# First feed-forward of a two-layer transformer step as one unrolled stream over the batches, its latents taken from the transposed normalised input

## The chip, the cores and the metric

The kernel runs on one core of a Trainium2 chip. The metric is device time in microseconds (us) of one launch. The times shown are the median of three runs and one profiled execution, from which every duration below is read.

## The reference, cut to what matters

The input x is 8 batches of 512 tokens of width 256. The layer adds to x an attention branch and a feed-forward branch, both fed by the layer norm of x. The attention branch norms its input a second time, scales and shifts it and projects it to two latents of width 128. A second layer (linear attention and routed experts) follows and isn't touched.

```
xn = _layernorm(x, axis=-1)
# attention branch, start (its input here is xn)
h = (x - mu) * jax.lax.rsqrt(var + LN_EPS) * ln_scale + ln_bias
c_q = h @ w_down_q.T
c_kv = h @ w_down_kv.T
# feed-forward branch
bw1 = _binarize(w1)          # mean |w| of each row times sign(w)
h = jnp.einsum('bsd,hd->bsh', x, bw1) + b1
h = jax.nn.gelu(h, approximate=False)
bw2 = _binarize(w2)
out = jnp.einsum('bsh,dh->bsd', h, bw2) + b2
```

## The kernel before

The program is a row of stages. Stage f (`stage_f`) comes first: for each batch b it computes `part` = x + xn + the feed-forward of xn, and the two latents, and writes both to HBM; stage a (`stage_a`, the attention) reads them. A barrier over all engines stands between the stages, so stage a starts its own loads only when stage f has ended.

The engines are TensorE (PE in the profile), VectorE (DVE), ScalarE (ACT), GpSimd (POOL) and SyncE (SP, which issues the loads and stores). Each runs its own instruction list in order and waits on semaphores. fp32 values that TensorE multiplies are split in a high part, rounded by ScalarE, and a low part, the rest, made by VectorE or GpSimd (`xT_hi`, `xT_lo`, `g_hi`, `g_lo`, `hT_hi`, `hT_lo`, `wd_hi`, `wd_lo`).

One batch, in `one(more)` of each engine, is:

- TensorE transposes h, the twice normed input, in 8 pieces into the banks `pX`; then 8 column blocks m of the up product, 4 matmuls each, into a ring of three banks `pU`; then the latents, 12 matmuls (`product`, lines 101 to 103), into `pX`; then the down product over 4 token tiles t, 64 matmuls of 256 columns (line 432) into two banks `pY`. At t = 2 it transposes the next batch's xn, for which it waits on the norm of that batch.
- ScalarE applies Gelu twice to each `pU` bank (into `g` and `g_hi`), rounds the latents, takes two square roots for the next batch's two norms (line 293), each behind the norm that feeds it, and rounds `xT_hi`. Square root and Gelu need different tables, each with a load.
- VectorE makes `hT` from the transposed h, the 8 `g_lo`, the latents' low parts, then the two norms of the next batch (`layer_norm`, lines 114 to 127), `xT_lo`, and, once the down product is there, `y` = `pY` times `alpha2` and `out` = `y` + `base`.
- GpSimd makes `base` = x + xn + b2 and splits hT.

There is one copy of each buffer. A batch ends in a meeting: each engine adds one to `arrived` and waits for `go` (`meet`); SP, which has issued the store of `part`, waits for all four and for the latents' store, clears 20-odd semaphores one by one and lets all go (`lead`, lines 90 to 97). The batches are a loop of seven turns and one copy behind it. Ahead of the loop all weights are loaded on one semaphore (`loaded`, 112), and signs and means are taken when the last has come. Behind it `part` of batch 7 is stored, and then a spare copy of latents 0 is made.

## Time and profile before

| | |
|---|---|
| median of 3 runs | 2234.28 us (2234.1 to 2235.52) |
| profiled execution | 2242.25 us, its span 2240.6 us |
| TensorE busy | 1922.1 us, 86% |
| VectorE busy | 1301.0 us, 58% |
| ScalarE busy | 895.0 us, 40% |
| GpSimd busy | 1328.1 us, 59% |
| mean granted TensorE clock | 0.94 of full |
| stage f | 0 to 277.31 us (the first load of stage a is issued then) |

Busy shares are means over stages with different limits; stage f takes an eighth of the span and is read by itself in the rows below. A row of the time line gives the start, the length, the engine, the line, the operation, what it writes and reads, and in brackets how long the engine had been idle and who released it. Matmuls overlap, so their pace is the distance of their starts, not their length. The granted clock is 1.00 at 2.4 GHz and 0.5 at 1.2 GHz.

### The profile page before, as it was taken

Reading aid. Unit: us, or ns where it says so; the run is one execution under the profiler, and the core shown is the slowest. Engines: PE = TensorE matmul, PEld = TensorE weight load, DVE = VectorE, ACT = ScalarE, POOL = GpSimd, SP = SyncE. Lnnn points to the kernel's source line nnn. Section 1 sums busy time; section 2 is a strip of 40 time slices with the busy share of each in tenths; the row PEclk is TensorE's granted clock in tenths of the full one; section 3 lists DMA queues with packets and bytes.
Section 4 is the critical chain, followed back from the end, with each engine's and each line's share of the span. In section 5 each row is a group of like instructions: output and inputs, shape, how many; then the busy total and the mean of one; then the engine's idle time right before and its main releaser. Section 6 shows DMA issues by size and latency. Waiting matters only on the chain. (4 is left out here: it accounts for less than half of the span.)

```text
span 2240.6 us, 35323 instructions
## 1 busy us (share of the span) xinstructions
PE 1922.1 (86%) x12804; PEld 1333.1 (59%) x12804; DVE 1301.0 (58%) x1857; ACT 895.0 (40%) x1536; POOL 1328.1 (59%) x860
## 2 busy tenths in 40 slices
PE   5777649999999999999999964888885699998798
PEld 4666524454454545454454533666764699998798
DVE  6666436666656565666656523676663466565343
ACT  4554324433434343433434212333321355554454
POOL 2333228886868687887878632544544566666533
PEclk9888869999999999999999977999997899999899
DMA  3212231323222231323232213122213433323122
GB/s 102 75 56 75 86 106 40 76 48 95 57 67 69 50 93 34 95 48 95 57 85 58 57 29 126 32 70 77 61 57 105 133 81 81 77 51 107 29 45 42
DMA packets 81606, 158.63 MB, mean 71 GB/s; under 512 B 14496, under 2 KB 63520, under 8 KB 75552
## 3 DMA queue, kind: packets, MB, share of 16 engines
q1 hardware_dynamic: 66464, 133.40, 21.2%
q0 software_dynamic: 14592, 18.40, 5.0%
q10 hardware_dynamic: 432, 5.24, 0.6%
q8 instruction: 76, 1.25, 0.2%
q14 instruction: 42, 0.34, 0.1%
HBM read 80.84 MB, written 44.17 MB: 56 GB/s over the span
## 5 line engine op out<-in xcount | busy, mean ns | idle before, releaser
L916 ACT ACTIVATE a_pr<-a_pT 128x1024 f32<-128x1024 f32 x256 | 262.1, 1024 | 432.4 <-PE a_pT L739 432.4
L949 POOL TENSOR_TENSOR a_total<-a_total,a_pr 128x1024 f32<-128x1024 f32 x128 | 321.0, 2507 | 149.9 <-ACT a_pr L916 149.5
L821 DVE TENSOR_REDUCE a_row_max<-a_pG 128x2 f32<-128x1024 f32 x256 | 309.2, 1220 | 148.7 <-PE a_pG L713 148.6
L1832 DVE TENSOR_TENSOR c_h_lo<-c_h,c_h_hi 128x256 fp32r<-128x256 f32 x288 | 213.0, 757 | 195.0 <-ACT c_h_hi L1811 176.9
L752 PE MATMUL a_pA<-a_pr,a_v 128*64 128x512 f32 x1024 | 277.0, 619 | 0.1
L1811 ACT ACTIVATE c_h<-c_pU,c_b_c 128x256 f32<-128x256 f32 x288 | 138.8, 482 | 235.1 <-PE c_pU L103 234.5
L949 POOL TENSOR_TENSOR a_total<-a_pr 128x1024 f32<-128x1024 f32 x64 | 151.7, 2370 | 59.7 <-ACT a_pr L916 59.5
L930 POOL TENSOR_TENSOR a_by_cos<-a_by_cos,a_swapped 128x1024 f32<-128x1024 f32 x64 | 155.1, 2424 | 46.3 <-DMA a_swapped<-a_by_sin 46.2
L815 DVE TENSOR_TENSOR a_by_sin<-a_pG,a_sin 128x1024 f32<-128x1024 f32 x64 | 78.4, 1225 | 141.9 <-PE a_pG L103 136.9
L937 POOL TENSOR_TENSOR a_qk_lo<-a_by_cos,a_qk_hi 128x1024 fp32r<-128x1024 f32 x64 | 158.9, 2483 | 2.3 <-ACT a_qk_hi L886 2.3
L1868 POOL DMA_INDIRECT out_x<-c_y,c_ids x72 | 114.7, 1593 | 41.4 <-DVE c_y L1840 22.7
L1811 ACT ACTIVATE c_h_hi<-c_pU,c_b_c 128x256 fp32r<-128x256 f32 x288 | 138.0, 479 | 0.0
L713 PEld LDWEIGHTS a_pG<-a_qk_hi 64*128 64x128 f32 x512 | 46.1, 187 | 150.4 <-issue 89.6
L770 PE MATMUL a_pG<-a_wo,a_att 128*128 128x256 f32 x512 | 119.9, 389 | 15.0 <-DVE a_att L842 15.0
L713 PE MATMUL a_pG<-a_qk_hi 64*128 64x512 f32 x512 | 121.3, 491 | 10.9 <-ACTq L897 6.4
L101 PE MATMUL c_pY<-d_w_hi,c_h_lo 128*128 128x256 f32 x368 | 107.0, 291 | 19.5 <-DVE c_h_lo L1832 18.8
L101 PE MATMUL c_pU<-c_xT_hi,d_w_lo 128*128 128x256 f32 x368 | 109.4, 297 | 12.2 <-remote 11.0
L886 ACT CAST a_qk_hi<-a_by_cos 128x1024 fp32r<-128x1024 f32 x64 | 67.1, 1048 | 126.7 <-POOL a_by_cos L930 126.7
L770 PEld LDWEIGHTS a_pG<-a_wo,a_att 128*128 128x128 f32 x512 | 96.1, 192 | 34.9 <-issue 19.3
L734 PE MATMUL a_pT<-a_qk_hi,a_qk_lo 64*128 64x512 f32 x512 | 113.1, 436 | 1.3 <-ACT a_pr L916 1.0
L273 POOL TENSOR_TENSOR f_base<-f_x_t,f_xn 128x1024 f32<-128x1024 f32 x8 | 18.9, 2363 | 151.2 <-SPq L96 151.2
L739 PE MATMUL a_pT<-a_neg_max,a_ones 64*128 64x512 f32 x512 | 108.3, 417 | 0.0
(248 smaller groups left out, 5072.7 us busy)
## 6 DMA issues: line engine op xcount, KB each, us to landing
a_swapped<-a_by_sin SPq DMA_DIRECT2D x256, 128.0 KB, 2.3
a_inv_by_head<-mid_inverses SPq DMA_DIRECT2D x32, 512.0 KB, 6.0
c_x_t<-mid_rows SPq DMA_DIRECT2D x37, 272.0 KB, 2.8
mid_latents<-f_c_parts SPq DMA_DIRECT2D x8, 1024.0 KB, 3.9
a_latent_parts<-mid_latents SPq DMA_DIRECT2D x8, 1024.0 KB, 7.2
d_raw<-in_weights SPq DMA_DIRECT2D x3, 2048.0 KB, 8.4
c_raw<-in_weights SPq DMA_DIRECT2D x3, 2048.0 KB, 8.1
f_x_t<-in_x SPq DMA_DIRECT2D x8, 512.0 KB, 3.9
```

Source lines behind the costliest of these rows:

```text
L101: nc.tensor.matmul(out, l_lo, r_hi, start=start, stop=False, **kw)
L713: last = nc.tensor.matmul(pair[:, h, :], qk_hi[rows, u % RQ, 0, t * P:(t + 1) * P], qk_hi[rows, u % RQ, 1, :], start=True, stop=True)
L752: last = nc.tensor.matmul(pA[64 * h:64 * h + 64, :], v[:, t, p, h, :], pr[:, n % RP, h, :], start=(t == 0), stop=(t == NT - 1))
L770: last = nc.tensor.matmul(pair[:, 0, 0:D], att[:, (NP * b + p) % RA, ts], wo[:, p * D:(p + 1) * D], start=(p == 0), stop=(p == NP - 1))
L821: nc.vector.reduce_max(row_max[:, u % 2, :, t], pair[:], AX.X).then_inc(read, 1)
L916: nc.scalar.activation(pr[:, n % RP, :, :], pT[:], ACT.Exp, scale=SCALE).then_inc(exp_done, 1)
L930: nc.gpsimd.tensor_tensor(by_cos[:, u % 2, :, :], by_cos[:, u % 2, :, :], swapped[:], ALU.add).then_inc(rope_done, 1)
L937: nc.gpsimd.tensor_tensor(qk_lo[:, u % RQ, :, :], by_cos[:, u % 2, :, :], qk_hi[:, u % RQ, :, :], ALU.subtract).then_inc(qk_lo_done, 1)
L949: nc.gpsimd.tensor_tensor(total[:, u % 2, :, :], before, pr[:, n % RP, :, :], ALU.add).then_inc(summed, 1)
L1811: nc.scalar.activation(dst[:, m % RH, :], pU[m % RH][:], ACT.Relu, bias=b1_c[:, e, m:m + 1]).then_inc(relu_done[m % RH], 1)
L1832: nc.vector.tensor_tensor(h_lo[:, m % RH, :], h[:, m % RH, :], h_hi[:, m % RH, :], ALU.subtract).then_inc(h_lo_done[m % RH], 1)
L1868: pool.indirect_dma_start(out=out, out_offset=bass.IndirectOffsetOnAxis(ap=ids[:, t:t + 1], axis=0), in_=y[:, t, :], in_offset=None, compu ...
```

## The change

Stage f is written out over the 8 batches with no loop and no meeting. Its semaphores are never cleared while it runs, but count up; VectorE clears all 50 of them at the start of stage a. Inputs, xn, the transposed halves, `g_lo`, `g_hi` and the latents have two buffers, `base` three, `out` four half batches; `g` becomes a ring of three blocks. TensorE alternates: after the up block m of batch b comes a half token tile of the down product of batch b - 1 (`down(b - 1, m)`, 8 matmuls).

The second norm is no longer computed over data. The mean of xn is zero and its variance is var/(var+eps), so h = xn times a number per token. Hence the latents are `wd` (multiplied by ln_scale, `wd_s`) times the xT halves that exist already, then multiplied by that number. The number must be laid along columns: GpSimd makes `diag` (identity times `rstd2[:, 1]`), TensorE multiplies a matrix of ones by it (`spread`, 4 fp32 matmuls), ScalarE copies the result (`cols`), VectorE multiplies (`scale`), and ScalarE and VectorE split the sum with the bias `c_bias`. Both square roots are one instruction (`roots`). What goes is the transposes of h, `hT` and its split. GpSimd takes over the addition that makes `out` (`result`). The loads of the weights are cut in halves with a semaphore each. The spare copy is made after batch 2.

```diff
-                        if t == 2 and more:
-                            pe.wait_ge(c_lo_done, 2)
-                            pe.wait_ge(ln_step, LN_ALL)
-                            transposes(xn, xT_done)
...
+            spent.append(st.lasting(name))
+            return spent[-1]
...
+        x_t = [sb(f"x_t{i}", [P, NT, D]) for i in range(2)]
+        xn = [sb(f"xn{i}", [P, NT, D]) for i in range(2)]
+        RB = 3
+        base = [sb(f"base{i}", [P, NT, D]) for i in range(RB)]
+        y = [sb(f"y{i}", [P, 2, D]) for i in range(2)]
+        RO = 4
+        out = [sb(f"out{i}", [P, 2, D]) for i in range(RO)]
...
+        RG = 3
+        g = sb("g", [P, RG, S])
...
+        pT = [bank(f"pT{c}") for c in range(KC)]
         pU = [bank(f"pU{i}") for i in range(3)]
         pY = [bank(f"pY{i}", (P, 2, D)) for i in range(2)]
+        pC = bank("pC")
...
+                sp.dma_start(x_t[0][:], tokens(x, 0)).then_inc(x_in[0], 16)
                 sp.dma_start(ident[:], ident_d).then_inc(ident_in, 16)
+                sp.dma_start(w1s[:, :, 0:half], turned[:, :, 0:half]).then_inc(w1s_in[0], 16)
+                sp.dma_start(w1r[:, 0:MC // 2, :], rows[:, 0:MC // 2, :]).then_inc(w1r_in[0], 16)
+                sp.dma_start(b1_c[:], b1).then_inc(b1_in, 16)
+                sp.dma_start(ln[:], ln_sb).then_inc(ln_in, 16)
+                sp.dma_start(wd[:], wd_t).then_inc(wd_in, 16)
+                sp.dma_start(w1s[:, :, half:], turned[:, :, half:]).then_inc(w1s_in[1], 16)
+                sp.dma_start(w1r[:, MC // 2:, :], rows[:, MC // 2:, :]).then_inc(w1r_in[1], 16)
+                sp.dma_start(x_t[1][:], tokens(x, 1)).then_inc(x_in[1], 16)
...
+                def spread_base(b):
+
+                    pool.wait_ge(norm, normed(b, ROOTS))
+                    if b:
+                        pool.wait_ge(spread_done, b)
+                    else:
+                        pool.wait_ge(ident_in, 16)
+                    for t in range(NT):
+                        nc.gpsimd.tensor_scalar(diag[:, t, :], ident[:], rstd2[:, 1, t:t + 1], None,
+                                                ALU.mult).then_inc(diag_done, 1)
+                    pool.wait_ge(norm, normed(b, XN))
+                    if b >= RB:
+                        pool.wait_ge(out_done, 2 * (b - RB) + 2)
+                    nc.gpsimd.tensor_tensor(base[b % RB][:], x_t[b % 2][:], xn[b % 2][:],
+                                            ALU.add).then_inc(sum_done, 1)
+                    if not b:
+                        pool.wait_ge(b2_in, 16 * NT)
+                    pool.wait_ge(sum_done, b + 1)
+                    nc.gpsimd.tensor_tensor(base[b % RB][:], base[b % RB][:], b2_rows[:],
+                                            ALU.add).then_inc(base_done, 1)
+
+                def result(q):
+                    b, i = q // 2, q % 2
+                    pool.wait_ge(y_done, q + 1)
+                    pool.wait_ge(base_done, b + 1)
+                    if q >= RO:
+                        pool.wait_ge(stored[q % RO], 16 * (q // RO))
+                    nc.gpsimd.tensor_tensor(out[q % RO][:], y[q % 2][:], base[b % RB][:, 2 * i:2 * i + 2, :],
+                                            ALU.add).then_inc(out_done, 1)
...
+                spread_base(0)
+                for b in range(B + 2):
+                    if b >= 2:
+                        result(2 * (b - 2) + 1)
+                    if b + 1 < B:
+                        spread_base(b + 1)
+                    if 1 <= b <= B:
+                        result(2 * (b - 1))
+                pool.wait_ge(out_done, 2 * B)
...
+                def roots(b):
+                    act.wait_ge(norm, normed(b, VAR2))
+                    nc.scalar.activation(std2[:], var2[:], ACT.Sqrt).then_inc(root, 1)
...
+                roots(0)
+                signs(0)
+                x_high(0)
+                act.wait_ge(b1_in, 16)
+                for b in range(B):
                     for m in range(MC):
+                        k = MC * b + m
...
+                        if k >= RG:
+                            act.wait_ge(g_lo_done, k + 1 - RG)
...
+                        if not b:
+                            if m == 0:
+                                signs(1)
+                            if m == 2:
+                                columns(0)
+                            if m == 4:
+                                act.wait_ge(w2s_in, 16)
+                                nc.scalar.activation(w2abs[:], w2s[:], ACT.Abs).then_inc(w2abs_done, 1)
+                            if m == 6:
+                                nc.scalar.activation(sign2[:], w2s[:], ACT.Sign).then_inc(sign2_done, 1)
+                        if b + 1 < B:
+                            if m == 0:
+                                roots(b + 1)
+                            if m == 4:
+                                x_high(b + 1)
+                            if m == 7:
+                                columns(b + 1)
+                        if m == 5:
+                            latent_high(b, 0)
+                        if m == 7:
+                            latent_high(b, 1)
...
+                def scale(b, i):
+                    dve.wait_ge(c_done, 2 * b + i + 1)
+                    dve.wait_ge(cols_done, b + 1)
+                    if b:
+                        dve.wait_ge(c_lo_done, 2 * b + i - 1)
+                    nc.vector.tensor_tensor(scaled[i][:], pC[:], cols[b % 2][:], ALU.mult).then_inc(scaled_done, 1)
+
+                def latent_low(b, i):
+                    dve.wait_ge(c_hi_done, 2 * b + i + 1)
+                    nc.vector.scalar_tensor_tensor(out=c_parts[b % 2][:, 2 + i, :], in0=scaled[i][:],
+                                                   scalar=c_bias[:, i:i + 1], in1=c_parts[b % 2][:, i, :],
+                                                   op0=ALU.add, op1=ALU.subtract).then_inc(c_lo_done, 1)
+
+                def weigh(q):
+                    dve.wait_ge(down_done, q + 1)
+                    if q >= 2:
+                        dve.wait_ge(out_done, q - 1)
+                    nc.vector.tensor_tensor(y[q % 2][:], pY[q % 2][:], alpha2[:], ALU.mult).then_inc(y_done, 1)
...
+                moments(0)
+                normalise(0)
+                means(0)
+                x_low(0)
+                moments(1)
+                means(1)
...
+                        if b >= 2 and m == 0:
+                            weigh(2 * (b - 2) + 1)
+                        if b + 1 < B and m == 1:
+                            normalise(b + 1)
+                        if m == 3:
+                            scale(b, 0)
+                        if b and m == 4:
+                            weigh(2 * (b - 1))
+                        if m == 5:
+                            if b + 1 < B:
+                                x_low(b + 1)
+                            latent_low(b, 0)
+                        if m == 6:
+                            scale(b, 1)
+                        if m == 7:
+                            latent_low(b, 1)
+                            if b + 2 < B:
+                                moments(b + 2)
...
+                def transposes(b):
+                    pe.wait_ge(norm, normed(b, XN))
+                    if b:
+                        pe.wait_ge(cols_done, b)
...
+                def spread(b):
+
+                    pe.wait_ge(diag_done, NT * (b + 1))
+                    pe.wait_ge(xT_lo_done, KC * b + 1)
+                    for t in range(NT):
+                        last = nc.tensor.matmul(pT[0][:, t * P:(t + 1) * P], ones[:], diag[:, t, :],
+                                                start=True, stop=True)
+                    last.then_inc(spread_done, 1)
...
+                        up(b, m)
+                        if b:
+                            down(b - 1, m)
+                        if not b and m == 0:
+                            pe.wait_ge(ln_in, 16)
+                            pe.wait_ge(wd_in, 16)
+                            for i in range(2):
+                                for c in range(KC):
+                                    last = nc.tensor.matmul(pC[:, i:i + 1], wd[:, (2 * c + i) * P:(2 * c + i + 1) * P],
+                                                            ln[:, 1, c:c + 1], start=(c == 0), stop=(c == KC - 1))
+                            last.then_inc(c_bias_made, 1)
+                            pe.wait_ge(ones_set, 1)
+                            spread(0)
+                        if m == 2:
+                            latents_of(b, 0)
+                        if b + 1 < B and m == 3:
+                            transposes(b + 1)
+                        if m == 5:
+                            latents_of(b, 1)
+                        if b + 1 < B and m == 6:
+                            spread(b + 1)
...
+                    for s in spent:
+                        dve.sem_clear(s)
```

The instructions as they now stand, at three places. VectorE before, the end of one batch and the start of the next (L367 makes `y`, L373 `out`, L87 is the meeting):

```order
L344 TENSOR_TENSOR f_xT_lo<-f_pX,f_xT_hi 128x512 [waits f_xT_hi_done] x2
L367 TENSOR_TENSOR f_y<-f_pY,f_alpha 128x512 [waits f_down_done,f_ln_step,f_xT_lo_done]
L367 TENSOR_TENSOR f_y<-f_pY,f_alpha 128x512 [waits f_down_done]
L373 TENSOR_TENSOR f_out<-f_y,f_base 128x512 [waits f_y_done,f_out_free,f_base_done]
L373 TENSOR_TENSOR f_out<-f_y,f_base 128x512 [waits f_y_done]
L87 ISA [waits f_out_done,f_c_lo_done,f_go1]
L392 REGISTER_ALU
L392 COMPARE_AND_BRANCH
L352 TENSOR_SCALAR f_hT<-f_pX,f_ln 128x512 [waits f_h_done] x2
L356 TENSOR_TENSOR f_g_lo<-f_g,f_g_hi 128x512 [waits f_gelu_done] x8
```

VectorE now, the first blocks of batch 3 (`f_g_lo1` is its low half, `f_y1` belongs to batch 1, `f_xn0` to batch 4):

```order
L526 TENSOR_TENSOR f_g_lo1<-f_g,f_g_hi1 128x512 [waits f_gelu_done]
L512 TENSOR_TENSOR f_y1<-f_pY1,f_alpha2 128x512 [waits f_out_done,f_down_done]
L526 TENSOR_TENSOR f_g_lo1<-f_g,f_g_hi1 128x512 [waits f_gelu_done]
L469 RECIPROCAL f_rstd2<-f_std2 128x8 [waits f_diag_done,f_root]
L471 SCALAR_TENSOR_TENSOR f_shift<-f_mean_var,f_rstd2 128x4 [waits f_norm]
L477 TENSOR_SCALAR f_xn0<-f_x_t0,f_rstd2,f_shift 128x256 [waits f_sum_done,f_norm]
L477 TENSOR_SCALAR f_xn0<-f_x_t0,f_rstd2,f_shift 128x256 x3
L526 TENSOR_TENSOR f_g_lo1<-f_g,f_g_hi1 128x512 [waits f_gelu_done] x2
L500 TENSOR_TENSOR f_scaled0<-f_pC,f_cols1 128x512 [waits f_c_lo_done,f_cols_done,f_c_done]
L526 TENSOR_TENSOR f_g_lo1<-f_g,f_g_hi1 128x512 [waits f_gelu_done]
```

The norm of the next batch stands between the second and third `g_lo`, no longer ahead of a meeting, and the out addition is gone from this engine.

TensorE before, from the end of the down product over the meeting to the next batch:

```order
L432 MATMUL f_pY<-f_sign,f_g_lo 128x256
L432 MATMUL f_pY<-f_sign,f_g_hi 128x256
L87 ISA [waits f_down_done,f_go0]
L453 REGISTER_ALU
L453 COMPARE_AND_BRANCH
L401 MATMUL f_pX<-f_ident,f_h 128x128 x8
L412 MATMUL f_pU<-f_xT_lo,f_sign 128x512
L413 MATMUL f_pU<-f_xT_hi,f_sign 128x512
L412 MATMUL f_pU<-f_xT_lo,f_sign 128x512
```

TensorE now, at the end of slot m = 3 of a batch:

```order
L272 MATMUL f_pY<-f_sign,f_g_lo 128x256
L272 MATMUL f_pY<-f_sign,f_g_hi 128x256
L569 MATMUL f_pT<-f_ident,f_xn 128x128 [waits f_cols_done,f_norm]
L569 MATMUL f_pT<-f_ident,f_xn 128x128 x7
L600 MATMUL f_pU<-f_xT_lo,f_sign 128x512 [waits f_gelu_done]
L601 MATMUL f_pU<-f_xT_hi,f_sign 128x512
L600 MATMUL f_pU<-f_xT_lo,f_sign 128x512
L601 MATMUL f_pU<-f_xT_hi,f_sign 128x512
L272 MATMUL f_pY<-f_sign,f_g_lo 128x256 [waits f_y_done]
```

The transposes of the next batch now stand between two up blocks, and wait for `norm` (xn ready).

ScalarE now, from the end of one batch (`cols` and the latents' second high part) over the start of the next:

```order
L392 COPY f_cols<-f_pT 128x512 [waits f_spread_done]
L398 ACTIVATE f_c_parts<-f_scaled,f_c_bias 128x512 [waits f_scaled_done]
L422 ACTIVATE f_g<-f_pU,f_b_c,f_alpha 128x512 [waits f_g_lo_done,f_up_done]
L422 ACTIVATE f_g_hi<-f_pU,f_b_c,f_alpha 128x512
L383 ACT_TABLE_LOAD
L383 ACTIVATE f_std<-f_var 128x8 [waits f_norm]
L422 ACT_TABLE_LOAD [waits f_g_lo_done]
L422 ACTIVATE f_g<-f_pU,f_b_c,f_alpha 128x512 [waits f_up_done]
L422 ACTIVATE f_g_hi<-f_pU,f_b_c,f_alpha 128x512
L422 ACTIVATE f_g<-f_pU,f_b_c,f_alpha 128x512 [waits f_g_lo_done,f_up_done]
```

The square root with its two table loads has moved from the end of the batch to between the first and the second Gelu pair.

## Rows read from the trace of the kernel before

**Rows 1.** Page, part 5: GpSimd's first instruction of each batch.

```profile
L273 POOL TENSOR_TENSOR f_base<-f_x_t,f_xn 128x1024 f32<-128x1024 f32 x8 | 18.9, 2363 | 151.2 <-SPq L96 151.2
```

**Rows 2.** Time line of PE, 88 to 125 us, one turn of the loop.

```profile
100.96 0.40 PE L101 MATMUL f_pX<-f_hT_hi,f_wd_lo 128*128 128x512 f32 x1
...
103.73 0.28 PE L432 MATMUL f_pY<-f_sign,f_g_lo 128*128 128x256 f32 x1
...
107.25 0.28 PE L432 MATMUL f_pY<-f_sign,f_g_hi 128*128 128x256 f32 x1
109.95 1.94 PE L401 MATMUL f_pX<-f_ident,f_xn 128*128 128x128 f32 x8 [2.43 <-DVE f_xn L127]
...
111.91 0.42 PE L432 MATMUL f_pY<-f_sign,f_g_hi 128*128 128x256 f32 x1
112.12 0.41 PE L432 MATMUL f_pY<-f_sign,f_g_lo 128*128 128x256 f32 x1
...
120.65 1.97 PE L401 MATMUL f_pX<-f_ident,f_h 128*128 128x128 f32 x8 [4.34 <-SPq L94]
```

**Rows 3.** Stage table: one turn; busy us, granted clock (PEclk).

```profile
120.60:151.60 31.00, 23.63 (x125) 19.82 (x126) 20.40 (x48) 15.98 (x25) 10.68 (x10) 0.89 0.19 70
```

**Rows 4.** Time line of PE, 20 to 32 us, ahead of batch 0.

```profile
20.68 5.56 PE L447 MATMUL f_pY<-f_w2abs,f_ones 128*128 128x256 f32 x16 [9.62 <-ACT f_w2abs L323]
28.65 1.07 PE L401 MATMUL f_pX<-f_ident,f_h 128*128 128x128 f32 x8 [2.42 <-SPq L94]
```

**Rows 5.** Time line of DVE, 90 to 126 us, same turn.

```profile
104.53 1.28 DVE L360 TENSOR_TENSOR f_c_parts<-f_pX,f_c_parts 128x512 fp32r<-128x512 f32 x2
105.73 1.40 DVE L114 BATCH_NORM_STATS2 f_stats<-f_x_t 128x6 f32<-128x256 f32 x4
...
108.43 1.38 DVE L127 TENSOR_SCALAR f_xn<-f_x_t,f_small 128x256 f32<-128x256 f32 x4
```

**Rows 6.** Time line of ACT, 90 to 126 us, same turn.

```profile
102.36 0.86 ACT L304 ACTIVATE f_g<-f_pU,f_b_c,f_alpha 128x512 f32<-128x512 f32 x1
103.03 0.86 ACT L304 ACTIVATE f_g_hi<-f_pU,f_b_c,f_alpha 128x512 fp32r<-128x512 f32 x1
...
104.87 1.28 ACT L293 ACT_TABLE_LOAD   x1
...
112.01 1.06 ACT L298 CAST f_xT_hi<-f_pX 128x512 fp32r<-128x512 f32 x2
```

**Rows 7.** f_g_lo by tile: count, then min/median/max ns.

```profile
L356 DVE TENSOR_TENSOR f_g_lo<-f_g,f_g_hi x64: 691/718/1840, 32.2 to 259.2; 128x512 fp32r<-128x512 f32 x64
```

**Rows 8.** Time line of DVE, 150 to 165 us.

```profile
157.60 1.04 DVE L356 TENSOR_TENSOR f_g_lo<-f_g,f_g_hi 128x512 fp32r<-128x512 f32 x1 [0.65 <-ACT f_g_hi L304]
```

**Rows 9.** Time line of POOL, 150 to 165 us.

```profile
154.49 1.29 POOL L278 TENSOR_TENSOR f_hT_lo<-f_hT,f_hT_hi 128x512 fp32r<-128x512 f32 x1
...
156.42 1.68 POOL L278 TENSOR_TENSOR f_hT_lo<-f_hT,f_hT_hi 128x512 fp32r<-128x512 f32 x1
```

**Rows 10.** Groups of POOL's instructions over the whole span.

```profile
L1590 POOL TENSOR_SCALAR d_own<-b_qT,b_own 128x512 f32<-128x512 f32 x32 | 50.4, 1587 | 16.0 <-DVE b_qT L1357 15.6
```

**Rows 11.** Time line of all engines, 0 to 29 us, start-up.

```profile
4.89 1.41 DVE L114 BATCH_NORM_STATS2 f_stats<-f_x_t 128x6 f32<-128x256 f32 x4 [4.89 <-DMA f_x_t<-in_x]
...
15.02 1.91 ACT L321 ACTIVATE f_sign<-f_w1s 128x2048 fp32r<-128x2048 f32 x1 [2.79 <-DMA f_ln<-in_ln_sb]
```

**Rows 12.** Time line of PE, 264 to 280 us.

```profile
266.17 0.28 PE L432 MATMUL f_pY<-f_sign,f_g_hi 128*128 128x256 f32 x1
```

**Rows 13.** Time line of SP, 264 to 280 us, the stage's end.

```profile
268.40 0.38 SPq L241 DMA_DIRECT2D mid_part<-f_out  x1
271.37 0.69 SPq L261 DMA_DIRECT2D mid_latents<-mid_latents  x1
277.31 0.37 SPq L520 DMA_DIRECT2D a_raw_q<-in_wq_t  x1
```

**Rows 14.** Time line of DVE, 276 to 300 us, its first work in stage a.

```profile
289.98 1.23 DVE L534 TENSOR_TENSOR a_wq_lo<-a_raw_q,a_wq_hi 128x1024 fp32r<-128x1024 f32 x1 [21.61 <-ACT a_wq_hi L528]
```

More of the change, by code:

```diff
@@ L184, in stage_f @@
[L184 to L189 removed]
+        inv_var = sb("inv_var", [P, NT])
+        share = sb("share", [P, NT])
+        var2 = sb("var2", [P, 2, NT])
+        std2 = sb("std2", [P, 2, NT])
+        rstd2 = sb("rstd2", [P, 2, NT])
+        shift = sb("shift", [P, NT])
+        xT_hi = [sb(f"xT_hi{i}", [P, KC, S], F32R) for i in range(2)]
@@ L251, in _ @@
[L251 to L261 removed]
+                half = FF // 2
@@ new lines, in up @@
+                def up(b, m):
+                    k = MC * b + m
+                    if k >= 3:
+                        pe.wait_ge(gelu_done, 2 * (k - 2))
+                    for c in range(KC):
+                        w = sign1[:, c, m * P:(m + 1) * P]
+                        nc.tensor.matmul(pU[k % 3][:], w, xT_lo[b % 2][:, c, :], start=(c == 0), stop=False)
+                        last = nc.tensor.matmul(pU[k % 3][:], w, xT_hi[b % 2][:, c, :], start=False,
+                                                stop=(c == KC - 1))
+                    last.then_inc(up_done, 1)
```

460 lines of the change are left out of this document (231 added, 229 removed).

## The prediction

> **What bounds the kernel now.** I read the page first. Its costliest groups are of later stages, but one row of stage f stands out: the first instruction of GpSimd in each batch had an idle time of 151.2 us before it in 8 times, and SyncE's line 96, the `go` of the meeting, ended it [rows 1]. So the stage is paced by its meetings, not by an engine. The stage table of one turn says the same: of 31.0 us TensorE is busy 23.6, VectorE 20.4, ScalarE 16.0, GpSimd 10.7, and TensorE's granted clock is 0.89 [rows 3]. Then the time line of TensorE over one turn. Two holes stand in it: 2.43 us for the norm of the next batch in the middle of the down product, and 4.34 us for the meeting [rows 2]. Behind the first hole the matmuls of 256 columns start 0.21 us apart (111.91 and 112.12), against 0.1135 before it (31 steps from 103.73 to 107.25): the lower of the two clock levels, 1.2 GHz.
>
> **The change, first a batch in the steady state.** What TensorE must do, at full clock. The 12 latent matmuls of 512 columns run from 100.96 to 103.73, 0.231 us each [rows 2]. The 32 up matmuls have that shape: 7.4 us. Down: 64 by 0.1135, 7.3 us. Latents: 2.8 us, as before. Transposes of xn: 8 took 1.07 us with their tail [rows 4], 0.85 net. Those of h (0.85) go. New is `spread`, 4 fp32 matmuls of 128 columns. Before has fp32 matmuls of 256 columns, 8 instructions (16 records) in 5.56 us [rows 4], 0.70 us each; half as many columns give 0.35 each, 1.4 us; at the best clock perhaps half. I take 0.9. Sum 19.3 us, with no hole in it. That is the floor of a batch.
>
> ScalarE: a Gelu is 0.67 us from start to start, 16 make 10.7; two table loads 1.28 each, 2.6; `xT_hi` 1.06 [rows 6]; three more passes of 512 columns at about 0.58, 1.7; the root 0.2. Sum 16.3.
>
> VectorE: 8 `g_lo` at 0.69 [rows 7] make 5.5; eight passes of the same size (`xT_lo`, `scale`, the latents' low part, `weigh`, two each), at 0.64 apart [rows 5], 5.1; statistics from 105.73 to the root, with two more tiny steps, 2.5; reciprocal, shift and xn 1.8 (1.38 of it xn [rows 5]). Sum 14.9. GpSimd: two additions of 1024 columns at 2.36 [rows 1], two of 512 at 1.29 [rows 9], and 4 `diag`; a tensor_scalar of 512 columns takes 1.59 [rows 10], so 128 columns about 0.45 and four 1.8. Sum 9.1. So TensorE is the engine with the most to do.
>
> But VectorE and GpSimd get in each other's way. A `g_lo` takes 0.69 us at best and up to 1.84 [rows 7]; the one at 157.60 took 1.04 and ended only 0.5 us after GpSimd's instruction of 156.42, which itself took 1.68 where its like at 154.49 took 1.29 [rows 8, 9]. I read: one waits for the whole instruction of the other. The Trainium skill says this outright (SBUF — State Buffer, section "SBUF: two separate sides"): the pair of ports that both share is an exclusive lock, and the one that comes second is blocked for a full instruction. By that rule the batch is the walk below, without it the floor of 19.3; the trace bears the lock out.
>
> Now walk one batch, time 0 at TensorE's first up block. A slot (up block, then half a down tile) is 0.93 + 0.91 = 1.84 us; latents (1.4) follow in slots 2 and 5, transposes in slot 3, `spread` in slot 6. ScalarE ends the previous batch at 1.6 (last Gelu pair 0.5, `cols`, latents). Then Gelu pair 0 to 2.9, load and root to 4.4, load to 5.7, pair 1 to 7.1. VectorE has finished the statistics of the batch after next meanwhile; `g_lo` 1 to 7.8, or 8.2 if the `out` addition (GpSimd, 6.3 to 7.6) holds it; then reciprocal, shift and xn to 10.2. TensorE wants to transpose at 3.68 + 1.84 + 1.4 + 1.84 = 8.8. **First stall: 1.4 us.** Behind xn come GpSimd's two additions of 2.36, with `g_lo` 2 and 3 squeezed in: `g_lo` 2 to 10.8, GpSimd to 13.2, `g_lo` 3 to 13.9, GpSimd to 16.2 (`scale` reads PSUM and goes through), `g_lo` 4 to 16.9, `weigh` to 17.5, `g_lo` 5 to 18.2, the first `xT_lo` to 18.9. TensorE wants `spread`, which overwrites the bank `xT_lo` reads, at 18.0. **Second stall: 0.9 us.** The rest fits: VectorE ends its last `g_lo` about 1.1 us into the next batch, as assumed. A batch is 19.3 + 1.4 + 0.9 = 21.6, with semaphore hops 21.8 us, against 31.0 now.
>
> The ring `g` of three blocks lets ScalarE be at most three ahead of VectorE; in the walk `g_lo` 3 is done at 13.9 and Gelu 6 comes at 17.1, so it isn't reached. Loads, stores and latents are issued on SP long before they are used.
>
> **The start.** x 0 has landed at 4.89, all the 4 MB of loads at 15.0 [rows 11]. The norm now takes the shorter way (one set of statistics): xn at 9.5, transposes to 11.2, `xT_hi` and `xT_lo` to 12.4 with half the signs in between. First up block 12.4 to 14.1 at the low clock, first Gelu 14.2. ScalarE then has the longest list: 8 Gelu pairs 10.7, signs and absolute values 1.91 each for a full matrix [rows 11], so half of sign1, `w2abs` and sign2 make 4.8, loads and root 2.8, `xT_hi`, `cols`, latents 2.8: 21 us, to 35. VectorE adds a latents part, statistics of batch 2 and `alpha2` behind it: 39.2. TensorE waits for `alpha2` there and starts batch 1's slots. x 1 is the ninth load (some 3.3 of 4 MB), so `g_lo` 0 starts only near 17.4; the ring of three covers it, barely. Before, batch 0 started at 28.65 [rows 4] and took a turn: 59.7.
>
> **The end.** Batches 1 to 6 are whole slots: 6 by 21.8 = 130.8, to 170.0. Batch 7 has no transposes, `spread` or norm: 18.5, to 188.5. Its down product stands alone, 7.3, after a wait of 1.3 for the last `g_lo`: 197.1. Then `weigh` 0.7, the addition on GpSimd 1.3, the store (268.40 to 271.37, 3.0 [rows 13]), 0.5 of hops and barrier: 202.6. Before, from TensorE's last matmul at 266.17 [rows 12] to stage a's first load at 277.31 [rows 13] it was 11.1, since the spare copy came behind the store (271.37 to 277.31, 5.9). The 50 semaphores that VectorE clears in stage a: a whole meeting with 23 clears kept TensorE idle 4.34 [rows 2], so 50 cost 9.4 at most; VectorE has nothing to do there from 277.31 to 289.98 [rows 13, 14], 12.7 us. Without that cover they would cost up to 9.4.
>
> **Sum.** 277.3 - 202.6 = 74.7 us off the profiled span of 2240.6: 2165.9, profiled time 2167.6. The profiled execution (2242.25) stood 8 us above the median of 2234.28, so I predict 2234.3 - 74.7 = 2159.6, 2160 us. Stage a begins behind a barrier, so nothing later changes, and nothing there gives it back.
>
> **The rivals.**
>
> *Floor* (0.27). The stalls are covered: the table loads fall in holes, or GpSimd's additions come late enough. Then a batch is 19.3 to 20.3, 6 of them 9 to 15 less: 2145 to 2151. For it: each stall is about 1 us in a walk of 20 steps. Against: the root, two loads and xn are one chain of over 6 us.
>
> *Clock* (0.19). TensorE falls to 1.2 GHz behind stalls. The evidence is split: a hole of 2.42 us at 28.65 left the 8 transposes at 1.07 us (full clock), one of 2.43 at 109.95 made them 1.94 and slowed what followed [rows 2, 4]. One fall costs 0.9 there and 7 matmuls by 0.1, about 1.6 us; one or two in each batch give 23.4 to 25, 6.5 batches by 1.6 to 3.2: 2170 to 2181. The Trainium skill (TensorE: Matmul & The Clock Gate, section "What's actually happening") says that the throttled state is the default and activity releases it, which speaks for a denser stream as good for the clock.
>
> *Slower* (0.03). The clock stays at 1.2 GHz through the stage, as alternating short groups with waits might do: 44 matmuls of 512 columns at twice 0.231, 64 at 0.213, transposes 1.9, `spread` 1.8: 37.6 us. Seven batches are 263; with 39.2 ahead, and 1.3, 14.0 and 5.5 behind, the stage ends at 323, 46 us later: 2280. It decides where 7 batches exceed 277.3 - 39.2 - 1.3 - 14.0 - 5.5 = 217, 31.0 us each.
>
> *No gain* (0.01). The stage is held by something unseen (a full ring, fetching a straight program): 31 us a batch. The waits named in the trace are all meeting and norm, which go.
>
> The rest (0.50) is my forecast, 21 to 23 us a batch, 2154 to 2168 alone. The start may be 5 us off either way, as all but its durations is reckoned. The range takes in floor and clock: 2141 to 2182. Within 0.2% (4.5 us) nothing could be told from no change; that and slower hold 0.04 together, faster 0.96.
>
> **What would show it.** Stage a's first load near 203 instead of 277; no idle time that SP ended in stage f; up blocks of one column block about 21.8 us apart; before the `f_xn` transposes an idle of 1 to 1.5 us ended by VectorE, before the `f_diag` matmuls about 1 us ended by `xT_lo`; `g_lo` longer on average than 0.93 us where it meets GpSimd; TensorE's clock 0.97 or more from 45 us on. I would be wrong if ScalarE's Gelu shows as what TensorE waits for, or if TensorE starts batch 1 much later than 39.

## The result, and the profile after

The changed kernel took 2168.36 us (median of four runs, 2162.8 to 2169.34), the kernel before 2234.19 beside it: a ratio of 0.970, 95% interval 0.9683 to 0.9717, so it is faster. 2160 was predicted, with 2141 to 2182 as the range. Of the 74.3 us forecast from the median, 65.8 came. The profiled execution took 2169.34 (span 2167.7), and its stage f ends, by stage a's first load, at 210.51 us instead of 277.31 [rows 13]: 66.8 us earlier, where 74.7 was predicted.

The stage table. Each row is a stretch: busy time and instructions of TensorE, its weight load, VectorE, ScalarE and GpSimd, then granted clock, DMA share and GB/s. The first two are the start, the third is batch 1, the fourth is one of the five batches behind it, which differ by less than 0.1 us, then batch 7 and the down product alone:

```profile
0.00:13.00 13.00, 1.94 (x8) 1.57 (x8) 6.90 (x22) 3.62 (x5) 4.10 (x9) 1.00 0.87 291
13.00:49.30 36.30, 24.60 (x92) 19.74 (x93) 20.94 (x49) 23.01 (x29) 15.04 (x13) 0.86 0.28 93
49.30:71.00 21.70, 21.54 (x125) 19.22 (x126) 13.46 (x19) 15.17 (x22) 9.91 (x7) 0.92 0.12 37
...
114.40:136.10 21.70, 19.96 (x125) 17.63 (x125) 15.67 (x34) 16.56 (x25) 11.44 (x8) 1.00 0.27 98
...
180.00:198.00 18.00, 18.00 (x114) 16.10 (x113) 10.01 (x14) 13.29 (x21) 3.10 (x2) 1.00 0.22 88
198.00:210.50 12.50, 7.41 (x61) 7.00 (x59) 3.35 (x5) 0.70 (x2) 3.82 (x3) 1.00 0.39 148
```

Against the turn of 31.0 us with clock 0.89 [rows 3], a batch is now 21.7 us with clock 1.00 (batch 1: 0.92), and TensorE is busy 92% of it. The 36.3 us of the second row are what went worse than forecast: TensorE stands idle 11.7 us there, at a clock of 0.86.

The time line of TensorE after, its stops in order: the start, one steady batch, the end. In brackets stand the idle time ahead and who ended it.

```profile
26.49 0.76 PE L101 MATMUL f_pC<-f_xT_hi,f_wd_lo 128*128 128x512 f32 x1 [5.46 <-DVE f_c_bias L530]
...
39.55 1.39 PE L578 MATMUL f_pT<-f_diag,f_ones 128*128 128x128 f32 x8 [3.42 <-DVE f_xT_lo L483]
...
42.44 4.24 PE L648 MATMUL f_pY<-f_w2abs,f_ones 128*128 128x256 f32 x16
49.32 0.47 PE L600 MATMUL f_pU<-f_xT_lo,f_sign 128*128 128x512 f32 x1 [2.64 <-issue]
...
103.32 1.09 PE L569 MATMUL f_pT<-f_ident,f_xn 128*128 128x128 f32 x8 [1.65 <-DVE f_xn L477]
...
111.14 0.28 PE L272 MATMUL f_pY<-f_sign,f_g_hi 128*128 128x256 f32 x1
111.51 1.13 PE L578 MATMUL f_pT<-f_diag,f_ones 128*128 128x128 f32 x8
...
179.61 0.40 PE L600 MATMUL f_pU<-f_xT_lo,f_sign 128*128 128x512 f32 x1
...
197.38 0.28 PE L272 MATMUL f_pY<-f_sign,f_g_lo 128*128 128x256 f32 x1
...
198.87 0.39 PE L272 MATMUL f_pY<-f_sign,f_g_lo 128*128 128x256 f32 x1 [0.37 <-DVE f_g_lo L526]
```

The holes of 2.43 and 4.34 us in each turn [rows 2] are gone, and no idle time on TensorE is ended by SP. Batch 1 begins at 49.32 and batch 7 at 179.61: six batches in 130.3 us, 21.7 each. The transposes after a stop of 1.65 us take 1.09 us, as at full clock [rows 4]. `spread` begins 0.37 us after the start of the last down matmul, some 0.25 more than the usual step of 0.12.

VectorE and GpSimd of the same batch:

```profile
100.78 0.69 DVE L526 TENSOR_TENSOR f_g_lo<-f_g,f_g_hi 128x512 fp32r<-128x512 f32 x1 [1.84 <-ACT f_g_hi L422]
...
101.83 1.44 DVE L477 TENSOR_SCALAR f_xn<-f_x_t,f_rstd,f_shift 128x256 f32<-128x256 f32 x4
...
106.85 1.08 DVE L526 TENSOR_TENSOR f_g_lo<-f_g,f_g_hi 128x512 fp32r<-128x512 f32 x1 [1.70 <-ACT f_g_hi L422]
...
109.17 1.60 DVE L526 TENSOR_TENSOR f_g_lo<-f_g,f_g_hi 128x512 fp32r<-128x512 f32 x1 [0.63 <-ACT f_g_hi L422]
```

```profile
101.69 3.34 POOL L336 TENSOR_SCALAR f_diag<-f_ident,f_rstd 128x128 f32<-128x128 f32 x4 [1.38 <-DVE f_rstd L469]
105.00 2.39 POOL L341 TENSOR_TENSOR f_base<-f_x_t,f_xn 128x1024 f32<-128x1024 f32 x1
107.46 2.75 POOL L346 TENSOR_TENSOR f_base<-f_base,f_b_rows 128x1024 f32<-128x1024 f32 x1
```

xn waits behind `g_lo` 1, which waits for Gelu pair 1: that is the 1.65 us stop. On ScalarE, Gelu pair 1 follows the square root, and the root itself stood 0.73 us for VectorE's statistics, which the walk took to be done by then:

```profile
97.78 0.21 ACT L383 ACTIVATE f_std<-f_var 128x8 f32<-128x8 f32 x1 [0.73 <-DVE f_var L463]
```

 The two longer `g_lo` end 0.5 to 0.6 us after GpSimd's additions (107.39, 110.21), not when their own 0.69 us would be over.

### The profile page after: what moved, and what is told of

Read it like the earlier page. It is cut to its first block and busy times, and to the rows that moved or that the text cites. A ratio compares the mean times of both kernels' runs of the same rounds, so it can differ in the third digit from the quotient of the medians.

```text
span 2167.7 us, 35007 instructions
## 1 busy us (share of the span) xinstructions
PE 1893.2 (87%) x12812; PEld 1316.4 (61%) x12812; DVE 1261.0 (58%) x1748; ACT 900.6 (42%) x1537; POOL 1331.8 (61%) x854
## 5 line engine op out<-in xcount | busy, mean ns | idle before, releaser
L101 PE MATMUL c_pY<-d_w_hi,c_h_lo 128*128 128x256 f32 x368 | 106.4, 289 | 19.3 <-DVE c_h_lo L2036 18.7
L974 PEld LDWEIGHTS a_pG<-a_wo,a_att 128*128 128x128 f32 x512 | 96.0, 192 | 34.9 <-issue 19.3
L102 PE MATMUL c_pU<-c_xT_lo,d_w_hi 128*128 128x256 f32 x368 | 106.4, 289 | 0.0
```

The source lines that it names most:

```text
L101: nc.tensor.matmul(out, l_lo, r_hi, start=start, stop=False, **kw)
L102: nc.tensor.matmul(out, l_hi, r_lo, start=False, stop=False, **kw)
L974: last = nc.tensor.matmul(pair[:, 0, 0:D], att[:, (NP * b + p) % RA, ts], wo[:, p * D:(p + 1) * D], start=(p == 0), stop=(p == NP - 1))
```

## The experiments

In each, the number to compare is stage a's first load, 210.51 us in the changed kernel. The later stages, which no experiment touches, take 1953.0 to 1959.4 us in the profiled executions of the experiments from e1 on (e3 aside), so the whole time says less. The first load is read from one execution of each kernel; TensorE's first transposes, ahead of every edit, begin between 9.56 and 9.76 us in all of them.

### e1: the norm one block earlier

```
-                        if b + 1 < B and m == 1:
+                        if b + 1 < B and m == 0:
                             normalise(b + 1)
```

> One edit to the changed kernel: VectorE's reciprocal, shift and xn of the next batch stand behind the first low half of a batch instead of behind the second, so they no longer wait for the second Gelu pair. Chain theory (TensorE's first stall is xn coming behind root, table load and Gelu pair 1): xn is ready 2 to 2.5 us earlier, the five idle times of 1.65 us before the xn transposes vanish, 8.2 us in all; stage a's first load at 202 to 203 us instead of 210.5, a batch 20.1 instead of 21.8. Rival (VectorE and GpSimd, which block each other, set the batch): xn comes earlier but the idle time moves to the spread matmuls, which wait for the low halves behind GpSimd's additions; a batch stays at 21 or more and stage a starts at 208 or later. Time against before: 0.966 by the first, 0.969 by the second.

Measured: 2160.8 us (five runs), ratio to before 0.9653 (0.9637 to 0.9669). Stage a begins at 206.09, 4.4 us earlier, between the theory and the rival. A batch is 20.8 us (101.41 to 122.18), and the start is 0.9 us longer (the wait for the bias is 6.13 us instead of 5.46). TensorE's stops in a batch:

```profile
101.41 1.09 PE L569 MATMUL f_pT<-f_ident,f_xn 128*128 128x128 f32 x8 [0.23 <-DVE f_xn L477]
110.06 1.13 PE L578 MATMUL f_pT<-f_diag,f_ones 128*128 128x128 f32 x8 [0.53 <-DVE f_xT_lo L483]
```

and why the second one came, on VectorE beside GpSimd:

```profile
98.61 1.26 DVE L471 SCALAR_TENSOR_TENSOR f_shift<-f_mean_var,f_rstd 128x4 f32<-128x4 f32 x1
...
107.27 2.05 DVE L526 TENSOR_TENSOR f_g_lo<-f_g,f_g_hi 128x512 fp32r<-128x512 f32 x1 [0.18 <-ACT f_g_hi L422]
109.24 1.28 DVE L483 TENSOR_TENSOR f_xT_lo<-f_pT,f_xT_hi 128x512 fp32r<-128x512 f32 x2
```

```profile
98.54 1.30 POOL L355 TENSOR_TENSOR f_out<-f_y,f_base 128x512 f32<-128x512 f32 x1 [8.86 <-DVE f_y L512]
...
106.02 2.74 POOL L346 TENSOR_TENSOR f_base<-f_base,f_b_rows 128x1024 f32<-128x1024 f32 x1
108.72 1.72 POOL L355 TENSOR_TENSOR f_out<-f_y,f_base 128x512 f32<-128x512 f32 x1
```

The first stall was the order of VectorE's list: it fell from 1.65 to 0.23 us. Some of it is given back. `f_shift`, 128 by 4 elements and 0.16 us otherwise, took 1.26 and ended with GpSimd's addition; and with everything earlier, `g_lo` 5 and behind it `xT_lo` now come late for `spread`, which is the forecast's second stall.

### e2: the copy of the bias two blocks earlier

```
-                        if not b and m == 2:
+                        if not b and m == 0:
                             dve.wait_ge(c_bias_made, 1)
```

> One edit to the changed kernel: in batch 0 VectorE copies c_bias behind the first low half, not behind the third. Start theory (TensorE's idle of 5.5 us at 21 to 26.5 us is the wait for this copy, since the latents' bank holds the bias until then): latents of batch 0 start near 21.5 instead of 26.5, and as ScalarE sat idle 5.7 us behind it, batch 1 starts 4 to 5 us earlier (44.5 to 45.5 instead of 49.3) and stage a at 205.5 to 206.5. Rival (ScalarE's list of 21 us sets the start): the hole is filled by ScalarE's own work, and less than 2 us comes of it.

Measured: 2159.23 us, one run; stage a at 204.22, 6.3 us earlier, more than either expected. The stop of 5.46 us ahead of the first latents is gone; batch 1 begins at 44.18 instead of 49.32 and meets its xn transposes at 53.67 instead of 59.83. Of these 6.2 us 5.1 come ahead of batch 1 and 1.0 in it, where the clock is now 1.00 and was 0.92. `spread` of batch 1 now waits 3.80 us for `xT_lo`.

### e3 and e3b: the sums of |w2| off the path

`w2abs` goes behind ScalarE's `xT_hi`; the sums go to the other transpose bank, so that batch 1's down product need not wait for them:

```
+                                if not b:
+                                    act.wait_ge(w2s_in, 16)
+                                    nc.scalar.activation(w2abs[:], w2s[:], ACT.Abs).then_inc(w2abs_done, 1)
...
-                            nc.vector.tensor_scalar(alpha2[:, i, :], pY[0][:, 0, :], 1.0 / FF, None,
+                            nc.vector.tensor_scalar(alpha2[:, i, :], pT[1][:, 0:D], 1.0 / FF, None,
...
-                        pe.wait_ge(alpha2_done, 2)
```

> Two edits in batch 0 of the changed kernel: the absolute values of w2 are taken behind the rounding of batch 1's transposed halves instead of ahead, and the 8 matmuls with ones that sum them go to a bank that isn't a down bank, so that TensorE waits for alpha2 only ahead of the next transposes. Start theory: the idle of 3.4 us ahead of spread shrinks by the 1.9 us of the absolute values, and the idle of 2.6 us ahead of batch 1 goes: 4 to 4.5 us, batch 1 at 45, stage a at 206 to 206.5. Rival: TensorE runs into ScalarE's Gelu list instead, and no more than 2 us comes of it.

Measured: 5632.22 us. This says nothing about the edit. The first instructions of TensorE, which are the same in both kernels and lie ahead of anything edited, were already slow; this is the row of e3:

```profile
9.67 3.37 PE L571 MATMUL f_pT<-f_ident,f_xn 128*128 128x128 f32 x8 [9.67 <-DVE f_xn L477]
```

The same eight took 1.94 us when the same kernel was run again:

> The same kernel as in e3_sums_aside, run once more, since there every matmul of the whole program, in stages the edit doesn't touch too, took 1.7 to 3 times as long, from the first transposes on (3.37 us for eight, 1.94 in the unedited kernel, whose instructions up to there are the same). If that belongs to the chip and not to the edit, the time is 2158 to 2168 and the expectations of e3_sums_aside hold: batch 1 at 45 and stage a at 206 to 206.5 (start theory), or less than 2 us gained (rival). If it belongs to the edit, it comes again.

Measured: 2164.16 us; stage a at 208.42, only 2.1 us earlier, as the rival said. The wait for `alpha2` is gone, the one for `xT_lo` is not. On TensorE, ScalarE and VectorE, in this order:

```profile
26.53 0.76 PE L101 MATMUL f_pC<-f_xT_hi,f_wd_lo 128*128 128x512 f32 x1 [4.56 <-DVE f_c_bias L530]
...
40.53 2.05 PE L580 MATMUL f_pT<-f_diag,f_ones 128*128 128x128 f32 x8 [3.80 <-DVE f_xT_lo L483]
```

```profile
34.84 1.07 ACT L388 CAST f_xT_hi<-f_pT 128x512 fp32r<-128x512 f32 x2
35.78 1.94 ACT L438 ACTIVATE f_w2abs<-f_w2s 128x2048 f32<-128x2048 f32 x1
...
38.26 0.80 ACT L422 ACTIVATE f_g_hi<-f_pU,f_b_c,f_alpha 128x512 fp32r<-128x512 f32 x1
```

```profile
39.09 0.69 DVE L526 TENSOR_TENSOR f_g_lo<-f_g,f_g_hi 128x512 fp32r<-128x512 f32 x1 [3.42 <-ACT f_g_hi L422]
39.70 1.28 DVE L483 TENSOR_TENSOR f_xT_lo<-f_pT,f_xT_hi 128x512 fp32r<-128x512 f32 x2
```

`xT_hi` is ready at 35.9, but on VectorE `xT_lo` stands behind `g_lo` 5, and that waits for Gelu pair 5. `w2abs` still stands ahead of that pair, so the edit moved it past `xT_hi` and left it in the way of `xT_lo`. Gelu pairs 3 and 4 ahead of it are late from the bias wait, which this edit leaves. e9 bears this out: it differs from e5 only in that `xT_lo` stands ahead of `g_lo` 5, and its `spread` of batch 1 waits for nothing where e5's waits 0.91 us.

### e4: the first half of the latents computed twice

```
-                    for c in range(KC):
+                    for c in [c for _ in range(times) for c in range(KC)]:
```

with `times` 2 in slot 2. TensorE does six more matmuls of 512 columns in each batch, with the same result.

> The changed kernel with the six matmuls of the first latent in slot 2 of each batch done twice (the second time they overwrite the first), 1.4 us more of TensorE in each batch and nothing else. Chain theory (TensorE waits 1.65 us for xn in slot 3): the 1.4 us vanish in that wait, which falls to 0.3, and a batch stays at 21.8; only batches 0, 1 and 7, which have no such wait, get longer, stage a at 212 to 214. Rival (the batch is set by TensorE's own work and the waits are caused by it): each batch gets 1.4 longer, 23.2, and stage a starts at 221 to 222.

Measured: 2174.02 us; stage a at 215.52, 5.0 us later. In the steady batches the stall before the transposes fell from 1.65 to 0.25 and the length stayed 21.73 (106.99 to 128.72):

```profile
106.99 1.09 PE L569 MATMUL f_pT<-f_ident,f_xn 128*128 128x128 f32 x8 [0.25 <-DVE f_xn L477]
...
128.72 1.09 PE L569 MATMUL f_pT<-f_ident,f_xn 128*128 128x128 f32 x8 [0.25 <-DVE f_xn L477]
```

So 1.4 us of TensorE's work cost nothing where the chain of root, Gelu, `g_lo` and xn set the pace. The 5.0 us lie in batches 0, 1 and 7, which have no such stall: TensorE's xn transposes come 4.0 us later in batch 1 (63.88 against 59.83), 3.6 later in batch 6 (172.19 against 168.55), and the rest comes behind them. Of the 4.0, 2.8 are the added matmuls; the other 1.2 come from longer waits and the clock of the start.

### e5: all three moves together

> The edits of e1, e2 and e3 together, all of them only places in the order. They gave or should give 4.4 (norm earlier, measured), 6.3 (bias copied earlier, measured) and 4 (sums aside, expected) us of stage f. If the start's waits are separate, they add: 14 to 15 us, stage a at 196, time 0.963 to 0.964 of before. Rival (in batch 0 each wait hides the next, ScalarE's list of 21 us is behind them all): stage a at 199 or later, and batch 1 starts no earlier than 41.

Measured: 2152.16 us (five runs), ratio to before 0.9616 (0.9597 to 0.9635). Stage a at 194.18: 16.3 us earlier, while the three alone give 4.4 + 6.3 + 2.1 = 12.8. The surplus lies in the start: batch 1's transposes begin at 48.35 instead of 59.83, 11.5 us earlier, while the three alone give 6.2 + 2.1 - 0.9 = 7.4. Two things differ there. Each wait had hidden part of the next: `spread` of batch 1 waits 0.91 us instead of the 3.80 of e2 and e3b. And TensorE's clock from 13 us to batch 1 is 1.00, against 0.86 in the changed kernel and in e1, 0.95 in e2 and 0.81 in e3b. No run parts the two. A new stop of 2.62 us is in it, ahead of the second latents: VectorE's `scale` stands behind two `g_lo` that take 5.49 us beside GpSimd's additions.

### e6: the down product apart

The loop over m again runs the up blocks alone, and the down product of the same batch follows; VectorE weighs both half batches in slot 4 of the next batch. The meetings and the second norm stay away:

```
                         up(b, m)
-                        if b:
-                            down(b - 1, m)
...
+                    for m in range(MC):
+                        down(b, m)
```

> The changed kernel without the interleave: TensorE does the eight up blocks of a batch, then the whole down product of the same batch, as before the change; VectorE weighs both half batches in the next batch's slot 4. Still no meetings, no second norm, no loop. Walk theory: while the up blocks run ScalarE sets the pace (16.3 us of list for 12 us of TensorE), then 7.5 us of down product with a wait of about 1.3 for the last low half ahead of its end: a batch of 24 to 26 us against 21.8, seven of them 15 to 30 us more: stage a at 225 to 240, time 0.976 to 0.984 of before. Rival (what the change gave is the meetings alone, the interleave is worth nothing): stage a at 212 or earlier.

Measured: 2228.28 us (ten runs), ratio 0.9962 (0.9948 to 0.9975). Both expectations failed: stage a begins at 275.42, where before it began at 277.31. The whole time is 9.5 us below that of the kernel before, measured beside it; only 1.9 of them lie in stage f of the profiled executions, and for the rest, in stages that the edit doesn't touch, no cause is shown. A batch is 30.8 to 32.4 us, 31.7 in the mean of five. TensorE in one of 30.8:

```profile
100.06 1.97 PE L568 MATMUL f_pT<-f_ident,f_xn 128*128 128x128 f32 x8 [4.14 <-DVE f_xn L477]
...
110.37 1.13 PE L577 MATMUL f_pT<-f_diag,f_ones 128*128 128x128 f32 x8 [2.71 <-DVE f_xT_lo L483]
...
114.69 0.38 PE L272 MATMUL f_pY<-f_sign,f_g_lo 128*128 128x256 f32 x1 [1.31 <-DVE f_g_lo L526]
```

Three stops in each batch, together 7.4 to 9.0 us. Five of the six first stops are followed by transposes of 1.97 us, the low clock; behind the sixth they take 1.09 and the up matmuls after them start 0.43 us apart, as at the low clock. The mean clock of a batch is 0.87 to 0.89 and TensorE is busy 23.3 us of it, where the changed kernel has 1.00 and 20.0. So of the 10 us by which a batch is longer than 21.7, some 6.6 are stops and 3.3 are the clock.

### e7: the interleaved kernel with the norm early and without b2

The kernel of e1, and GpSimd's addition of b2 is left out (`part` lacks b2, and with it all that follows from it).

> The kernel of e1 (norm early) without GpSimd's second addition of 1024 columns in each batch: b2 is left out of the result. Lock theory (what took back half of e1's gain is VectorE's low halves 4 and 5 standing behind GpSimd's additions, 1.5 and 2.05 us instead of 0.69): the low halves ahead of spread fall to near 0.69 to 1.0, the idle of 0.53 us ahead of spread goes, a batch is 20.2 instead of 20.8, stage a at 202.5 to 203.5 instead of 206.1. Rival (another chain, ScalarE's list or the bank ring, sets the batch at 20.8): stage a stays at 205.5 to 206.5 although the low halves are short.

Measured: 2165.06 us, one run; stage a at 203.96, 2.1 us before e1 (theory 2.6 to 3.6 before it, rival about none). The wait of `spread` fell from 0.53 to 0.21 us, a batch from 20.8 to 20.5, and `g_lo` 5 from 2.05 to 1.74: GpSimd's next addition moved up and held it instead. The theory holds at rather over half its size.

### e8: apart, with the norm early

e6 and the edit of e1.

> The down product apart, as in e6_apart, and the norm of the next batch taken after the first g_lo instead of the second. Theory (in e6_apart TensorE waits because the chain of ScalarE's root, Gelu pair 1, its g_lo and xn is longer than the four up blocks and the latents that stand beside it, and the waiting then costs TensorE its clock): VectorE can begin the norm at the root, 94.74 in e6_apart, instead of behind Gelu pair 1 and its g_lo at 98.1, 3.4 us earlier, so the stall of 4.14 before the transposes falls to under 1 us, the transposes take about 1.1 instead of 1.97 us and the clock stays up. A batch of 32.2 us becomes 27.5 to 28.7, and stage a starts near 245 to 252 instead of 275.4. Rival (another list, not the xn chain, holds the batch apart, and what the norm gives is waited for at the spread or at the down product): a batch of 31 or more, stage a at 267 or later.

Measured: 2222.74 us, one run; stage a at 262.13, and batches of 28.6 to 29.7 us, 29.2 in the mean of five: somewhat above the theory's, and the stage between the two. TensorE:

```profile
95.32 1.09 PE L568 MATMUL f_pT<-f_ident,f_xn 128*128 128x128 f32 x8 [0.78 <-DVE f_xn L477]
103.04 0.80 PE L101 MATMUL f_pC<-f_xT_hi,f_wd_lo 128*128 128x512 f32 x1 [4.34 <-DVE f_scaled L500]
```

VectorE and GpSimd in that gap:

```profile
97.48 4.90 DVE L526 TENSOR_TENSOR f_g_lo<-f_g,f_g_hi 128x512 fp32r<-128x512 f32 x2 [0.64 <-ACT f_g_hi L422]
102.31 0.68 DVE L500 TENSOR_TENSOR f_scaled<-f_pC,f_cols 128x512 f32<-128x512 f32 x1
```

```profile
96.28 2.80 POOL L341 TENSOR_TENSOR f_base<-f_x_t,f_xn 128x1024 f32<-128x1024 f32 x1
99.16 2.67 POOL L346 TENSOR_TENSOR f_base<-f_base,f_b_rows 128x1024 f32<-128x1024 f32 x1
```

The xn stall fell from 4.14 to 0.78 and the transposes took 1.09 us, as the theory said. A new wait of 4.34 us took over part of it. Two `g_lo` that need 1.38 us took 4.90, one behind each of GpSimd's additions, and TensorE's second latents waited behind them for `scale` to free the bank `pC`.

### e9: all moves, and `xT_lo` ahead of the weighing

```
+                        if b + 1 < B and m == 4:
+                            x_low(b + 1)
                         if b and m == 4:
                             weigh(2 * (b - 1))
                         if m == 5:
-                            if b + 1 < B:
-                                x_low(b + 1)
```

> All three moves of e5_all_moves, and the low half of the transposed xn taken by VectorE right behind g_lo 4, ahead of the weighing and of g_lo 5. Theory (what is left in a steady batch is the 0.53 us that spread waits for xT_lo, and VectorE reaches it late only because of its order): the two passes start at 94.5 instead of 97.3 in the batch of 93 to 114, spread waits for nothing, and a batch of 20.8 becomes 20.3: stage a at 191 to 192 instead of 194.2, ratio to before 0.960 to 0.961. Rival (the weighing and GpSimd's out addition behind it come later by 1.3 us, and hold VectorE's next g_lo or the bank that the down product wants): no gain, stage a at 193.5 or later.

Measured: 2149.44 us (five runs), ratio 0.9601 (0.9579 to 0.9622), the lowest of all, though its interval overlaps e5's. Stage a at 188.78, 5.4 us before e5, twice the forecast: a batch is 0.8 us shorter where 0.5 was reckoned, and 1.1 come in batch 0. `spread` waits for nothing, and a batch is 20.0 us:

```profile
107.16 1.09 PE L571 MATMUL f_pT<-f_ident,f_xn 128*128 128x128 f32 x8 [0.23 <-DVE f_xn L477]
115.11 1.06 PE L580 MATMUL f_pT<-f_diag,f_ones 128*128 128x128 f32 x8
127.17 1.09 PE L571 MATMUL f_pT<-f_ident,f_xn 128*128 128x128 f32 x8 [0.23 <-DVE f_xn L477]
```

Stage f is 21.7 us shorter than in the changed kernel, from the order of the lists and one other bank alone.

## Why the prediction was right, and where it was off

**The steady batch.** 21.8 forecast, 21.7 measured, and the nearness is in part luck. TensorE's work without its stops is 19.8 us where the floor said 19.3, and the hops took up 0.2 of that: a slot is 1.87 us, not 1.84, and the first matmul behind each fp32 group starts late. The two stalls together came out as 1.9 us where 2.3 was forecast, 1.65 and about 0.25 instead of 1.4 and 0.9. The first is shown by e1 (an order on VectorE) and e4 (TensorE has 1.4 us to spare there). The second grows to 0.53 when the first is gone (e1), and its cause is that `xT_lo` comes late behind GpSimd's additions and VectorE's own order (e7, e9).

**The lock.** Two `g_lo` that take 1.38 us by themselves took 4.90 beside GpSimd's additions of 2.80 and 2.67 (e8). This bears out the rule of the Trainium skill (SBUF — State Buffer, section "SBUF: two separate sides") on which the walk rested, that the pair of ports which both engines share is an exclusive lock, held for a whole instruction. The sign that I gave, more than 0.93 us for a `g_lo` that meets GpSimd, held: the two of the eight in the batch shown that meet an addition took 1.08 and 1.60. Over all of them, from 49 to 200 us, the mean is 0.88 (49.3 us for 56).

**GpSimd's `diag`.** I estimated 0.45 us for each and 9.1 a batch; they took 0.84 (3.34 for four), and GpSimd 11.4. The extra 1.5 us put both additions later, so that they meet `g_lo` 4 and 5 and not 2 and 3 as in the walk; what that cost or saved no run shows.

**The start: the step that failed.** "TensorE waits for `alpha2` there and starts batch 1's slots" at 39.2; it was 49.32, 10.1 us late, and a start much later than 39 was a sign of being wrong that the prediction itself had named. I had added up ScalarE's list as if it never waited. Its work was priced nearly rightly (21.8 us for 21). It began 2.3 us late, at 16.50: the first load of Gelu's table, 1.28 us, came behind the first up block and was in no sum, and that block was 1.0 late. And it waited 7.0 us between the first Gelu and the end of its list, 5.7 of them at 30.72, because TensorE stood 5.46 us for `c_bias`:

```profile
30.72 0.78 ACT L422 ACTIVATE f_g<-f_pU,f_b_c,f_alpha 128x512 f32<-128x512 f32 x1 [5.74 <-PE f_pU L601]
```

The bias product and the latents share the bank `pC`, and VectorE copied the bias out only after two more `g_lo` and a norm. Then `xT_lo` was late by 3.4 us, behind `w2abs`, Gelu pair 5 and `g_lo` 5, and `alpha2` by 2.6, as VectorE took the statistics of batch 2 first. Behind the stops the matmuls ran at the low clock in part (0.86 in the mean; the sums over `w2abs` 4.24 us, and 3.61 in e5 with the clock at 1.00). I had named those instructions, but not put them in the order of the banks that they share. e2 shows the first wait worth 6.3 us; e5, with the sums and the norm moved too, takes batch 1's transposes 11.5 us forward.

The lock also held a tiny instruction, for which I had no term. On VectorE, and GpSimd beside it, in the changed kernel:

```profile
15.52 2.31 DVE L461 TENSOR_TENSOR f_share<-f_mean_var,f_inv_var 128x4 f32<-128x4 f32 x1
...
23.20 0.69 DVE L526 TENSOR_TENSOR f_g_lo<-f_g,f_g_hi 128x512 fp32r<-128x512 f32 x1 [2.25 <-ACT f_g_hi L422]
...
119.12 0.16 DVE L461 TENSOR_TENSOR f_share<-f_mean_var,f_inv_var 128x4 f32<-128x4 f32 x1
```

```profile
15.46 2.35 POOL L341 TENSOR_TENSOR f_base<-f_x_t,f_xn 128x1024 f32<-128x1024 f32 x1
```

It is no part of the 10.1 us: VectorE was idle 2.25 us ahead of `g_lo` 1, for ScalarE, before it came to the bias. Only where the copy stands behind `g_lo` 0, as in e2 and e5, does the delay reach it (TensorE still waits 0.61 us for `c_bias` in e5).

**The end.** It gives a little back. The six batches took 130.3 us (130.8 forecast); batch 7 17.8 (18.5), from 179.61 to 197.38, where its own down product begins; that product with its wait 8.2 (8.6), to 205.6; and the rest to stage a's load 4.9 (5.5). So 202.6 + 10.1 - 0.5 - 0.7 - 0.4 - 0.6 = 210.5. The 50 clears stayed under the loads: VectorE's first work in stage a begins 12.2 us after the first load, and before it was 12.7.

**The rivals.** Floor did not come, even in e9 (20.0 us) only its upper edge. Clock did not come in the steady batches: stops of 1.65 us left it at 1.00. It did come in the start (0.86, and 0.92 in batch 1). All six stops of 4.13 and 4.14 us in e6 were followed by matmuls at the low clock, those of 4.34 in e8 by a first matmul of 0.80 us instead of 0.40. For shorter stops the length alone does not decide: before, five of the seven stops of 2.43 to 2.45 us were followed by the low clock and two (at 203.21 and 234.29) were not.

**What the prediction did not see.** It named the meetings and the norm as what paces the stage, and gave the interleaving no price of its own. e6 takes both away and keeps only 1.9 of the 66.8 us; with these lists the interleaving brings the rest, for it covers the chains (root, Gelu, xn; `xT_hi`, `xT_lo`) that are as long without the meetings, and keeps TensorE's clock up. The lists of e6 were ordered for the interleaved stream, and one reordering (e8) takes 13.3 us off it; with the same reordering the interleaved kernel (e1) is still 56.0 us ahead (206.09 against 262.13). How good the best separate order would be stays open.
